# Four weight buffers on one queue, and copies of the down projections on VectorE, in an attention and mixture-of-experts layer on eight cores

## What is computed

```
q_lat, k_lat, v_lat = x @ Wq_down, x @ Wk_down, x @ Wv_down     # 16 heads x 64
q = concat(q_lat @ Wq_up_c, rope(q_lat @ Wq_up_e));  k likewise;  v = v_lat @ Wv_up
y = softmax(causal(q k^T / 8)) v @ Wc
x = layernorm(x + y)
gating = softmax over the two largest of (x @ Wg^T)              # 0 for the other experts
hidden = silu(x @ W1^T) * (x @ W2^T)                             # for all 8 experts
ffn = sum over experts of gating * (hidden @ W3^T)
out = layernorm(x + ffn)
```

## Time and profile before

| | us |
|---|---|
| median of 2 runs | 8245.58 |
| lowest and highest | 8204.45, 8286.71 |
| the profiled execution | 8101.59 |
| its span on core 0, the slowest | 8100.0 |
| its spans on the 8 cores | 8039.4 to 8100.0 |
| TensorE busy with matmuls on core 0 | 5534.6 (68%) |
| VectorE, ScalarE, POOL busy | 1300.0, 890.3, 745.2 |

### The profile page before, as it was taken

How to read it: one execution, slowest core, us unless ns; L and a number is a source line. 1 busy time by engine, 2 the same in 40 slices (tenths; PEclk the granted TensorE clock), 3 DMA queues, 4 the chain that set the end, 5 groups by cost and what they waited for, 6 DMA issues and landing times.

```text
span 8100.0 us, 59059 instructions; the slowest of 8 cores (8039.4 to 8100.0 us)
## 1 busy us (share of the span) xinstructions
PE 5534.6 (68%) x20398; PEld 2097.2 (26%) x20398; DVE 1300.0 (16%) x2448; ACT 890.3 (11%) x1171; POOL 745.2 (9%) x1151
## 2 busy tenths in 40 slices
PE   5667755446457767777777777777777777777784
PEld 1221111111122223223222333233233322223331
DVE  2430000000531111111111111111111111111113
ACT  0013322223000000000000000000000000000000
POOL 1011111100000000000000000000000000000000
PEclk7665555555779999989999999987799999998976
DMA  4269999950123333333333333333333333333332
GB/s 80 42 136 202 216 211 213 215 125 18 37 60 96 99 99 101 101 95 96 99 99 101 97 101 102 94 96 94 96 97 98 102 99 93 98 99 94 101 97 89
DMA packets 635179, 868.16 MB, mean 107 GB/s; under 512 B 62976, under 2 KB 425728, under 8 KB 634640
## 3 DMA queue, kind: packets, MB, share of 16 engines
q0 software_dynamic: 159840, 428.10, 24.4%
q1 hardware_dynamic: 475056, 436.28, 17.1%
HBM read 866.32 MB, written 146.80 MB: 125 GB/s over the span
## 4 chain that ended last, share of the span: by engine, by line
DMA 46%; PE 38%; issue 9%; DVE 5%; ACT 2%; DVEq 0%; POOLq 0%; SPq 0%; POOL 0%; ACTq 0%
PE pS L847 29%; DMA w12s<-w12b 21%; DMA w3s<-w3b 12%; PE px L847 9%; DMA w12b<-wtb 4%; DMA wtb<-w12i 3%; DMA wtb<-w3p 3%; DMA w3b<-wtb 2%; DVE rbuf L847 1%; ACT attTA L847 1%; DVE cbuf L847 1%; DMA wstage<-wq 1%; DVE lnm L847 1%; DVE V L847 1%; DVE oac L847 0%
## 5 line engine op out<-in xcount | busy, mean ns | idle before, releaser
L847 PE MATMUL pS<-uA,w12s 128*128 128x512 bf16 x5632 | 1517.9, 418 | 847.8 <-DMA w12s<-w12b 814.5
L847 PE MATMUL pS<-x1te,w12s 128*128 128x512 bf16 x5632 | 1436.2, 401 | 0.0
L847 PE MATMUL pS<-w3s,hiddenG 128*128 128x512 bf16 x2816 | 780.2, 402 | 603.9 <-DMA w3s<-w3b 561.9
L847 PEld LDWEIGHTS pS<-uA,w12s 128*128 128x128 bf16 x5632 | 559.4, 104 | 1717.8 <-issue 1299.9
L847 ACT ACTIVATE s1b<-pS 128x512 bf16<-128x512 f32 x704 | 420.3, 597 | 5192.3 <-PE pS L847 5192.3
L847 DVE TENSOR_TENSOR hiddenG<-s1b,pS 128x512 bf16<-128x512 bf16 x704 | 483.6, 687 | 3019.8 <-PE pS L847 3019.8
L847 PEld LDWEIGHTS pS<-x1te,w12s 128*128 128x128 bf16 x5632 | 583.1, 104 | 774.3 <-issue 283.2
L847 PE MATMUL px<-w3s,hiddenG 128*128 128x512 bf16 x2816 | 781.7, 403 | 0.0
L847 POOL DMA_DIRECT2D w12s<-w12b x352 | 311.9, 886 | 3118.7 <-PE pS L847 2692.1
L847 PEld LDWEIGHTS pS<-w3s,hiddenG 128*128 128x128 bf16 x2816 | 261.4, 101 | 1075.1 <-issue 893.8
L847 PE MATMUL px<-attTA,V 128*65 128x512 bf16 x640 | 290.1, 606 | 333.6 <-DVE ytmp L847 283.5
(11 more groups left out here) (97 smaller groups left out, 1810.1 us busy)
## 6 DMA issues: line engine op xcount, KB each, us to landing
w12s<-w12b SPq DMA_DIRECT2D x352, 512.0 KB, 4.1
w12s<-w12b POOLq DMA_DIRECT2D x352, 512.0 KB, 4.7
w3s<-w3b SPq DMA_DIRECT2D x352, 256.0 KB, 3.0
w3s<-w3b POOLq DMA_DIRECT2D x352, 256.0 KB, 2.9
wtb<-w12i POOLq DMA_DIRECT2D x234, 384.0 KB, 8.0
w12b<-wtb SPq DMA_DIRECT2D x234, 384.0 KB, 6.2
wtb<-w3p POOLq DMA_DIRECT2D x117, 384.0 KB, 8.0
w3b<-wtb SPq DMA_DIRECT2D x117, 384.0 KB, 6.4
```

What stands on the lines that cost most here:

```text
L847: inst = getattr(engine, meth)(*a, **k)
```

## The change

It has five parts:

- `w12s` has four buffers in place of two, and all its loads go to SP's queue. All loads of `w3s` (still two buffers) go to POOL's queue. The PSUM banks of a step follow the buffer number, now 0 to 3, so they are b1 = 0 to 3 and b2 = 2 to 5. `s1b` stays at two.
- The copies of the down projections go from ScalarE to VectorE, and use banks 0 and 1 alone.
- `gTrow`, `gRow` and the ones of that matmul are bf16 in place of f32.
- `outb` has one buffer, and its wait stands ahead of a block's first instruction.
- Semaphores for the new buffers.

```
-                b = (0, 1, 6, 7)[tc]
+                b = tc % 2
...
-                S.wait("scalar", "sp", mm)
-                last_ev = S.op("scalar", "copy",
+                S.wait("vector", "sp", mm)
+                last_ev = S.op("vector", "tensor_copy",
                                A5[:, fp, tc * 512:(tc + 1) * 512], pf[b][:, :],
-                               inc="ss")
-                S.bank_free(b, "ss", last_ev)
+                               inc="sv")
+                S.bank_free(b, "sv", last_ev)
...
-    gTrow = es_f.enter_context(nc.sbuf_tensor("gTrow", [8, NTB, 128], F32, side="right"))
-    gRow = es_f.enter_context(nc.sbuf_tensor("gRow", [1, 2, 512], F32, side="right"))
+    gTrow = es_f.enter_context(nc.sbuf_tensor("gTrow", [8, NTB, 128], BF16, side="right"))
+    gRow = es_f.enter_context(nc.sbuf_tensor("gRow", [1, 2, 512], BF16, side="right"))
...
-    w12s = es_f.enter_context(nc.sbuf_tensor("w12s", [128, 2, NCT, 2, 128], BF16, side="right"))
+    w12s = es_f.enter_context(nc.sbuf_tensor("w12s", [128, 4, NCT, 2, 128], BF16, side="right"))
...
-    outb = es_f.enter_context(nc.sbuf_tensor("outb", [128, 2, 1024], F32))
+    outb = es_f.enter_context(nc.sbuf_tensor("outb", [128, 1, 1024], F32))
...
     def w12_load(e, ts, ht):
-        buf = ht % 2
-        q = "sync" if buf == 0 else "gpsimd"
-        S.slot_wait(q, ("w12s", buf))
+        buf = ht % 4
+        S.slot_wait("sync", ("w12s", buf))
...
-        m_w12[(e, ts, ht)] = S.dma(q, dstb, srcb, f"rl{buf}")
+        m_w12[(e, ts, ht)] = S.dma("sync", dstb, srcb, f"rl{buf}")
...
     def w3_load(e, ts, ht):
         buf = ht % 2
-        q = "gpsimd" if buf == 0 else "sync"
-        S.slot_wait(q, ("w3s", buf))
+        S.slot_wait("gpsimd", ("w3s", buf))
...
-        mgbm = S.op("tensor", "matmul", pf[b][:, :], lhsT=ones1[0:1, 0:128],
+        mgbm = S.op("tensor", "matmul", pf[b][:, :], lhsT=ones_bf[0:1, :],
...
             for ht in range(NHT):
-                buf = ht % 2
+                buf = ht % 4
...
-        S.slot_wait("vector", ("outb", tb % 2))
+        S.slot_wait("vector", ("outb",))
```

More of the change, by code:

```diff
@@ L148, in build @@
     bk = es_all.enter_context(nc.sbuf_tensor("bk", [128, 128], BF16))
+    ones_bf = es_all.enter_context(nc.sbuf_tensor("ones_bf", [1, 128], BF16))
     wvup = es_all.enter_context(nc.sbuf_tensor("wvup", [128, 64], BF16))
@@ L185, in build @@
     S.op("gpsimd", "memset", ones1[:], 1.0)
+    S.op("gpsimd", "memset", ones_bf[:], 1.0)
     S.op("gpsimd", "memset", cshift[:], -20.0, inc="sq")
@@ L304, in up_proj_rope @@
     def up_proj_rope(pi, bmat, scale):
-        S.wait("tensor", "ss", m_lat_last[pi])
+        S.wait("tensor", "sv", m_lat_last[pi])
         dst = QT if pi == 0 else KT
@@ L342, in build @@
     up_proj_rope(0, bq, SCALE)
-    S.wait("scalar", "sp", S.cnt["sp"])
+    S.wait("vector", "sp", S.cnt["sp"])
     down_proj(1, d["wk"], 8)
     mk_done = up_proj_rope(1, bk, 1.0)
-    S.wait("scalar", "sp", S.cnt["sp"])
+    S.wait("vector", "sp", S.cnt["sp"])
     down_proj(2, d["wv"], 16)
@@ L352, in build @@
          inc="sv")
-    S.wait("tensor", "ss", m_lat_last[2])
+    S.wait("tensor", "sv", m_lat_last[2])
     for h in range(NH):
@@ L683, in w12_load @@
         dstb = w12s[:, buf].rearrange("p ct m h -> p ct (m h)")
-        m_w12[(e, ts, ht)] = S.dma(q, dstb, srcb, f"rl{buf}")
+        m_w12[(e, ts, ht)] = S.dma("sync", dstb, srcb, f"rl{buf}")
     def w3_load(e, ts, ht):
         buf = ht % 2
-        q = "gpsimd" if buf == 0 else "sync"
-        S.slot_wait(q, ("w3s", buf))
+        S.slot_wait("gpsimd", ("w3s", buf))
         m_w3[(e, ts, ht)] = S.dma(
-            q, w3s[:, buf, :],
+            "gpsimd", w3s[:, buf, :],
             d["w3b"][e, ht * 128:(ht + 1) * 128, :], f"u{buf}")
@@ L757, in build @@
                 S.wait("scalar", "sp", mm1)
-                S.slot_wait("scalar", ("s1b", buf))
-                ms1 = S.op("scalar", "activation", s1b[:, buf, :],
+                S.slot_wait("scalar", ("s1b", ht % 2))
+                ms1 = S.op("scalar", "activation", s1b[:, ht % 2, :],
                            pf[b1][:, :], AF.Silu, inc="ss")
@@ L764, in build @@
                 mhg[ht] = S.op("vector", "tensor_mul", hiddenG[:, ht, :],
-                               s1b[:, buf, :], pf[b2][:, :], inc="sv")
-                S.slot_set(("s1b", buf), "sv", mhg[ht])
+                               s1b[:, ht % 2, :], pf[b2][:, :], inc="sv")
+                S.slot_set(("s1b", ht % 2), "sv", mhg[ht])
                 S.bank_free(b2, "sv", mhg[ht])
@@ L830, in build @@
         S.wait("vector", "ss", mrstd)
-        mo = S.op("vector", "tensor_scalar_mul", outb[:, tb % 2, :], cbuf[:],
+        mo = S.op("vector", "tensor_scalar_mul", outb[:, 0, :], cbuf[:],
                   lnr[:, 0:1], inc="sv")
@@ L834, in build @@
         mdma = S.dma("sync", d["out"][tb * 128:(tb + 1) * 128, :],
-                     outb[:, tb % 2, :], f"so{tb % 2}")
-        S.slot_set(("outb", tb % 2), f"so{tb % 2}", mdma)
+                     outb[:, 0, :], f"so{tb % 2}")
+        S.slot_set(("outb",), f"so{tb % 2}", mdma)
     S.wait("sync", "so0", S.cnt["so0"])
```

## The result

| | before | after |
|---|---|---|
| median, us | 8178.15 (10 runs) | 7143.11 (11 runs) |
| lowest and highest, us | 8086.25, 8315.58 | 7098.04, 7425.93 |
| the profiled execution, us | 8101.59 | 7145.5 |
| its slowest core | core 0, 8100.0 | core 0, 7144.0 |
| ratio of the times | | 0.8761, 95% interval 0.873 to 0.8792 |

The changed kernel is faster by 12.4%. In some executions of the kernels here one die shows a lower granted clock (4 of 12 recorded for the changed kernel, the longest 7425.93 us); ratios and the times given for experiments are without those that it makes clearly longer.

The account below looks back on a forecast made before the run. TensorE's waits for w12 (814.5 us) and w3 (561.9 us) slices were taken as the bound. Full clock gave 8101.6 - 1138 + 42 = 7006 us; low clock added 0.85 x 689, making 7592, given as 7600; range 7100 to 7720.

Parts of the forecast that it names:

- the share of the low clock: FFN on the slowest core: TensorE at about 0.81 clock in some 85% of it, adding 0.85 x 689 us.
- The sum at full clock: Whole kernel with TensorE at full clock throughout the FFN: 8101.6 - 1138 + 42 = 7006 us.
- the second rival: Whole kernel: clock stays as profiled, low in a quarter of the FFN or less, 7006 to 7180 us; chance 0.20.
- up part and bridge: First pieces of each of 32 FFN passes: 22 steps of 3.45 us without w12 waits, 75.9, then 1.9 us.
- down part: w3 matmuls of each FFN pass: still bound by refilling two buffers, 60.1 us unchanged, plus 1 us (0 to 3).
- end of a pass: Between FFN passes: next w12 slice already there, only VectorE's accumulation is awaited, 0.8 us in place of 7.65.
- change of expert: At 7 FFN pass ends TensorE waits for x1te, made by VectorE after the accumulation; 8.7 us each, stays.
- half speed after stops: FFN: matmul groups that begin at half speed after the 7 stops at changes of expert, 20 us in all.
- last LayerNorm: With one outb the wait precedes the reduction: 2.8 us later in 15 of 16 blocks, 42 us more.
- the third rival: w12 loads: SP's queue serves slices one by one; 7464 us (0.03), or in the slower form 8942 us (0.02).
- the fourth: Up part: waits go but contention keeps steps near the old length, only pass ends are won, about 7980 us; chance 0.03.
- the collision with the w12 slices: Start of the down part: first new w3 load meets the last of the next pass's w12 loads, 1 us (0 to 3).

Follow-up runs that it names:

- The two runs: Changed kernel with two w12 buffers and the new queues, 7493.97 us; changed kernel with four w12 buffers and the old mixed queues, 7358.26 us.
- run 4: Not a run number: "in another run 4 and 5" means cores 4 and 5, in the changed kernel with down-projection copies back on ScalarE in four banks, 7137.26 us.

## Why the prediction was right and where it failed

**The step that failed is the share of the low clock.** The forecast took 0.81 in 85% of the FFN, 586 us, and reached this from the median of two unprofiled runs: 144 us above the profiled execution, read as an execution with the low clock in nearly all of the FFN. The profile after has 0.98 over the FFN (0.96 to 1.00 pass by pass) and 1.00 in the up part, and no pass of it at 0.81. The sum at full clock, 7006 us, was nearer to the result than the forecast, and the second rival (clock as profiled, 7006 to 7180, given 0.20) is what happened.

The inference was weak at its root. Where the clocks of the two dies of the kernel before lie within 0.008 of each other (12 executions), it took 8120 to 8232 us, 8186 in the middle. One of the two unprofiled runs, 8204.45, lies in there, and the profiled execution, 8101.59, below all of them: it was a quick one, and more than half of the 144 us is ordinary spread. The count of passes was high as well: window by window six passes of core 0 have a clock of 0.80 to 0.85, and not about 8.

There was better evidence in the trace of before. The row of core 4 that the prediction names for its die isn't among; with that of core 0 it is:

```profile
60.00:100.00 40.00, 37.08 (x170) 16.09 (x169) 0.00 (x0) 12.29 (x21) 7.22 (x10) 1.00 0.85 141
...
60.00:100.00 40.00, 39.25 (x179) 17.55 (x181) 0.00 (x0) 13.66 (x24) 7.23 (x10) 1.00 0.93 152
```

Core 0 stands first, core 4 second; core 2 had 0.81 in the same 40 us. All eight cores were dense there (37 to 40 us busy), cores 2 and 3 had 0.81, and the other six 1.00, cores 0 and 1 of the same die among them. From 5502 to 5684 it was the other way round: cores 0 and 1 had 0.79, cores 2 and 3 0.94 and 0.95. So density alone doesn't bring the low clock; what brings it stays open.

The Trainium skill's rule of 13/16 (TensorE: Matmul & The Clock Gate, section "Seeing it yourself"), by which a whole die goes there once three of its cores run dense matmuls, did not hold in these traces: in the profile before only two cores of a die had it in either window, and in the profile after eight cores with up parts of 76 us without a pause kept a mean clock of 0.835 to 0.842 over their spans, idle stretches included.

The 0.91 of the FFN before came in part from the low clock on core 0 (0.79 in the earlier trace rows) and in part from the 71 steps at half speed and the ends of the passes, whose next 8 matmuls took 3.57 us. On core 4 the second part alone gave 0.94.

**That the range held is in part luck.** The sum at full clock, 7006 us, lies below the range. What carried the profiled execution to 7145.5 is a late start of the FFN (79 us), which no term held, and 59 us in the FFN. Without the late start core 0 would have ended at 7067 us, and the four cores that began early did end at 7050 to 7065, below the lower bound of 7100.

The sum at full clock against the measured terms, core 0:

| step | predicted | measured |
|---|---|---|
| up part and bridge, a pass | 75.9 + 1.9 | 78.5 (77.9 to 80.6) |
| down part, a pass | 61.1 | 62.9 |
| end of a pass, 24 | 0.8 | 0.84 |
| change of expert, 7 | 8.7 | 8.66 |
| half speed after stops, 8 passes | 20 in all | 16, within the 78.5 |
| FFN | 4545 | 4604 |
| last LayerNorm | +42 | +43.7 |
| start of the FFN | 0 | +79 |

The measured length after the FFN is 137.7 us (7006.31 to 7144.0) and was 94.0 (8006.03 to 8100.0). The LayerNorm term was right in size and in place. The sum closes: 7006 + 59 + 79 + 2 = 7146.

**Up part, right.** Steps of 3.45 us, no wait for w12, one queue carries the slices; the third rival (a queue that serves one slice after another) and the fourth (the steps stay long) are refuted by the same rows. The DMA share rose from 0.39 to 0.49, not to 0.53. The reason, that the buffers cover the refill, holds: four of them with the old queues give 80.3 us. What the text didn't see is that the new queues alone give much of it too (91.6), since SP refills a buffer 0.84 us sooner and the steps at half speed go, and that a third buffer would have been enough.

**Bridge, right:** from the matmul of the gate row, now one pass of 0.39 us, to the first w3 matmul it is 1.85 us (2761.12 to 2762.97), for 1.9.

**Down part, unchanged in kind, short by 1.8 us a pass, 56 us in all.** Half of that is in the starting value. The 60.1 us were read from one pass, and the mean of the 32 passes in the same trace is 61.0. I had taken 1 us for the collision with the w12 slices asked for at its start. In the profile after the waits for w3 in the first 7 us of a down part average 2.1 us, before 1.1; that 1 us is there. The other 0.9 us a pass is spread over the later pairs. With two w12 buffers and the new queues the down part took 60.9 us, and with three 63.0. So the extra goes with the deeper prefetch or with the spread of executions; one profile each doesn't separate them.

**End of a pass, right in size.** The 0.84 us came as said. The prediction has both causes in one sentence, the loads that run ahead and that nothing of w3 stands between them, and I did not weigh them; what I expected of the run with the old queues shows that I counted on the free buffers. The two runs show that the second is what counts: a w3 load in front of the w12 slices on SP held them.

**Start of the FFN, missing.** The 79 us are no effect of the change as far as the runs show; they are a spread between executions and cores that one profile can't reveal. The forecast's arithmetic from one profiled execution carries this uncertainty, up to 80 us.

## What to carry to other kernels

Where a loop waits for a buffer to be refilled, count three things apart: how many steps lie over a refill, how long the issuing engine takes from the release to the landing, and what stands in front of the load on its queue. Undo each alone before you share out a gain: here more buffers were worth 13 us a pass in the up part with the new queues and 29 with the old, and the new queues 17 with two buffers and 2 with four. Only the order in the queue, 7 us at each end of a pass, was out of the buffers' reach. When one part of a loop is cured, look at once for the same pattern in the next part: a third buffer for w3 gave 20 us a pass. And don't read a state of the clock out of a median that has no clock beside it.

## What the runs showed of the hardware that I had not expected

- From the release of a buffer to its first use after a refill of 512 KB, in the rows shown: 4.78 us when SP issues (0.24 to the issue), 5.62 us when POOL does (0.72). With two buffers for w12 this made an up part of 91.6 or 106.7 us.
- TensorE's granted clock in the FFN rose from 0.94 (core 4, before) to 0.98 (core 0, after) as the engine became denser. In the kernel before, whose waits for w12 have a mean of 1.8 us, 71 of them were followed by steps that began at half speed; with w12 on SP and two buffers, a mean of 0.87 us, one was.
- The clock of 0.79 to 0.81 came on two neighbouring cores at a time in the profile before (2 and 3 from 60 to 100 us, 0 and 1 from 5502 to 5684), beside 0.94 to 1.00 on the other two of the same die.
- Cores end a stage whose transfer engines are full at 0.94 to 0.96 at times that differ by up to 80 us, mostly two neighbours together (0 and 1, 6 and 7; in another run 4 and 5), and differently in each execution.
